# Latent loads split between two blocks, expert rows gathered in the second attention, x quantised beside weight products, row statistics counted with the residual adds: one change to a four-layer decoder on one core

## The reference, cut to what matters

```
x = x + L0_attn(layernorm(x), ...)            # linear attention with decay
x = x + L0_xattn(layernorm(x), ctx_512, ...)  # attention over a latent context
x = x + L0_ffn(layernorm(x), ...)             # reordered, fp8-quantised FFN
x = x + L1_attn(...)                          # selective scan
x = x + L1_xattn(layernorm(x), ctx_512, Wq, w_kc_q, w_kc_kv, W_qr, W_kr, Wo)
x = x + L1_ffn(...)                           # mixture of 8 experts
x = x + L2_attn(...)                          # gated delta rule
x = x + L2_xattn(...)                         # same form as L1_xattn
x = x + L2_ffn(...)                           # 2:4 sparsified FFN
x = x + L3_attn(...)                          # differential attention
x = x + L3_xattn(...)
x = x + L3_ffn(...)                           # shared FFN and 8 experts
```

```
xr = (x / scale)[:, up_index]                     # columns reordered
scale_x = max|xr| per row / 448;  qx = fp8(xr / scale_x)
Wr = W[:, idx];  w_scale = max|Wr| per row / 448;  qw = fp8(Wr / w_scale)
y = qx * scale_x @ (qw * w_scale).T * scale       # gate and up, then down;
                                                  # gate and up outputs are taken at down_index
```

```
q_big = (x @ Wq.T per head) @ w_kc_q              # 128 -> 192 for each head
q_r, k_r = q_big @ W_qr, kv_rope @ W_kr;  attn = softmax(q_r @ k_r.T)
out = ((attn @ kv_rope) @ w_kc_kv.T per head) @ Wo.T
```

## Time and profile before

| | |
|---|---|
| median of 3 runs | 3720.2 us (3717.62 to 3721.66) |
| the profiled execution's own time | 3713.15 us, granted clock 0.84 |
| its span (first to last instruction) | 3711.4 us |
| PE busy | 2790.7 us, 75% of the span |
| PE weight loads | 1860.7 us, 50% (beside PE) |
| DVE busy | 2208.6 us, 60% |
| ACT busy | 1084.3 us, 29% |
| POOL busy | 482.0 us, 13% |
| moved by DMA | 70.29 MB, 19 GB/s on average; 41997 of 85585 packets under 512 B |

### The profile page before, as it was taken

How to read it: one execution, slowest core, us unless ns; L and a number is a source line. 1 busy time by engine, 2 the same in 40 slices (tenths; PEclk the granted TensorE clock), 3 DMA queues, 4 the chain that set the end, 5 groups by cost and what they waited for, 6 DMA issues and landing times. The chain is left out here.

```text
span 3711.4 us, 49035 instructions
## 1 busy us (share of the span) xinstructions
PE 2790.7 (75%) x19853; PEld 1860.7 (50%) x19854; DVE 2208.6 (60%) x4259; ACT 1084.3 (29%) x2461; POOL 482.0 (13%) x321
## 2 busy tenths in 40 slices
PE   4683343649988896698698698695888763898999
PEld 2452321233324564595595695694436742535555
DVE  3555686943369427677677676672494654395233
ACT  2150012510048313233133123221483111384111
POOL 0002000200036222000000000000262000163000
PEclk8896556769999897799799799797799965799899
DMA  5001000040000102000000000004000004001100
GB/s 105 1 1 33 0 3 0 0 107 0 0 1 2 47 0 96 1 1 1 1 1 1 1 2 1 1 1 102 1 2 35 1 16 101 2 2 30 42 1 12
DMA packets 85585, 70.29 MB, mean 19 GB/s; under 512 B 41997, under 2 KB 80334, under 8 KB 84782
## 3 DMA queue, kind: packets, MB, share of 16 engines
q1 hardware_dynamic: 80349, 63.49, 7.0%
q10 hardware_dynamic: 3984, 2.20, 0.3%
q0 software_dynamic: 1024, 1.45, 0.1%
HBM read 56.65 MB, written 4.19 MB: 16 GB/s over the span
## 5 line engine op out<-in xcount | busy, mean ns | idle before, releaser
L1769 POOL TENSOR_SCALAR work<-work,small 128x512 f32<-128x512 f32 x192 | 300.5, 1565 | 1173.0 <-DVE small L1729 1172.9
L1679 PE MATMUL psum<-keysT,arena_a 64*128 64x512 f32 x768 | 237.9, 700 | 65.5 <-ACT work L1793 62.7
L1793 ACT ACTIVATE work<-psum,small 128x512 f32<-128x512 f32 x384 | 261.9, 692 | 73.6 <-DVE small L1723 73.6
L1723 DVE TENSOR_REDUCE small<-psum 128x2 f32<-128x1024 f32 x192 | 230.9, 1204 | 31.2 <-PE psum L1679 25.4
L2867 ACT ACTIVATE work<-psum 128x256 f32<-128x256 f32 x320 | 95.5, 411 | 288.0 <-PE psum L2774 287.0
L1679 PEld LDWEIGHTS psum<-keysT,arena_a 64*128 64x128 f32 x768 | 62.6, 198 | 182.1 <-ACT work L1793 137.3
L2848 DVE TENSOR_TENSOR work<-psum,work 128x256 f32<-128x256 f32 x256 | 108.7, 425 | 74.7 <-PE psum L2802 69.8
L1597 DVE TENSOR_TENSOR arena_a<-psum,work 96x512 f32<-96x512 f32 x96 | 62.8, 681 | 146.0 <-PE psum L1563 146.0
L1346 PE MATMUL psum<-arena_b,arena_a 96*96 96x512 f32 x128 | 94.1, 907 | 72.6 <-DVE arena_b L1375 38.2
L2774 PE MATMUL psum<-consts,work 128*128 128x128 f32 x640 | 83.4, 288 | 76.1 <-DVE work L2839 76.1
L1776 ACT ACTIVATE work<-work,small 128x512 f32<-128x512 f32 x192 | 139.1, 726 | 0.0
(11 more groups left out here) (552 smaller groups left out, 5961.9 us busy)
## 6 DMA issues: line engine op xcount, KB each, us to landing
arena_a<-in_L_xattn_Wo SPq DMA_DIRECT2D x3, 2048.0 KB, 13.2
arena_a<-in_L_xattn_Wq SPq DMA_DIRECT2D x3, 2048.0 KB, 20.8
work<-keys SPq DMA_DIRECT2D x48, 128.0 KB, 5.1
arena_a<-in_L_xattn_w_kc_q SPq DMA_DIRECT2D x3, 1536.0 KB, 16.5
arena_a<-in_L_attn_w_qkv SPq DMA_DIRECT2D x1, 4096.0 KB, 13.6
decay_rows<-work SPq DMA_DIRECT2D x2, 1532.0 KB
arena_b<-in_L_ffn_We_gate_up SPq DMA_DIRECT2D x1, 2816.0 KB
arena_a<-in_L_xattn_W_qr SPq DMA_DIRECT2D x3, 768.0 KB, 4.4
```

The source lines that it names most:

```text
L1679: mm = nc.tensor.matmul(ps[:, m % 2 * 2 + j, :], qT[r:r + DC, i, t * P:(t + 1) * P], k.keysT[r:r + DC, b * SK:(b + 1) * SK], start=True, s ...
L1723: nc.vector.tensor_reduce(top[:, 2 * m:2 * m + 2], ps[:, m % 2 * 2:m % 2 * 2 + 2, :], AX.X, ALU.max, negate=True).then_inc(*maxed.up())
L1769: nc.gpsimd.tensor_scalar(e, e, total[:, 2 * m:2 * m + 1], None, ALU.mult).then_inc(*even_scaled.up())
L1793: last = nc.scalar.activation(probs[m % 4][:, j, :], ps[:, m % 2 * 2 + j, :], ACT.Exp, bias=top[:, 2 * m + j:2 * m + j + 1], accum_out=tot ...
```

## The change

1. **Latent loads.** `latent_attention` issues W_qr, W_kr, w_kc_kv, Wo and w_kc_q in the layernorm's block and the rest (Wq, the sine and cosine tables of layer 1, keys4) in the fold block. keys4 is laid out so that each of its 16 DMAs moves 4 KB runs (32x1024) instead of 256 B runs (32x16x64).
2. **l3_ffn's large loads** ("l3f") are issued in the block of `route`.
3. **Expert rows.** The two short index lists are loaded in L0_xattn's first block and `gather` runs on POOL in L0_xattn's second block; the gathered rows (wgu) lie in arena_a now, the diagonals in arena_b.
4. **x is quantised** by DVE in the weights' block, between L1004 and L1007, and the small block is dissolved into it.
5. **Row statistics** are also counted at the end of L0_attn, L0_xattn, L1_ffn, L2_ffn and L3_attn (`count_rows`, `close_rows`), whose residual adds go by tiles of 256 columns instead of 512 (in three of them), and the layernorms behind them are `counted`. ACT loads the square root's table ahead of time at the end of L0_xattn, L1_ffn and L2_ffn.

```diff
+def count_rows(k, dve, added, t):
+    dve.wait_ge(*added.at(t + 1))
+    row_stats(k, t).then_inc(*k.sig("rowed").up())
+
+def close_rows(k, dve):
+    dve.wait_ge(*k.sig("rowed").at(NT))
+    for t in range(NT):
+        k.nc.vector.bn_aggr(k.ln_mv[:, t, :], k.ln_two[:, t, :])
...
@@ def l0_xattn(k, lists, gather):
+        @block.sync
+        def _(sp):
+            lists(sp)
...
+        @block.gpsimd
+        def _(pool):
+            gather(pool)
...
+        @block.scalar
+        def _(act):
+            nc.scalar.activation(k.ln_rs[:, 1, 0:1], k.c["one"], ACT.Sqrt)
...
-            for b in range(B):
+            for t in range(NT):
+                b = t // 2
                 dve.wait_ge(*mm_out.at(b + 1))
-                nc.vector.tensor_tensor(x[:, 2 * b:2 * b + 2, :], x[:, 2 * b:2 * b + 2, :],
-                                        ps[:, b, :].rearrange("p (t d) -> p t d", t=2), ALU.add)
+                nc.vector.tensor_tensor(x[:, t, :], x[:, t, :], ps[:, b, t % 2 * D:(t % 2 + 1) * D],
+                                        ALU.add).then_inc(*added.up())
+                if t >= 1:
+                    count_rows(k, dve, added, t - 1)
+            count_rows(k, dve, added, NT - 1)
+            close_rows(k, dve)
...
@@ l1_ffn, behind each residual add of the last expert
+                if e == E - 1:
+                    dve.wait_ge(*added.at(g + 1))
+                    row_stats(k, t).then_inc(*k.sig("rowed").up())
+            close_rows(k, dve)
...
@@ l0_ffn
-    diag = A.take(P, 18, P)
-    wgu = Bq.take(FP, 2 * FT, D)
+    wgu = A.take(FP, 2 * FT, D)
+    diag = Bq.take(P, 18, P)
...
+            k.link(dve, nc.vector.tensor_tensor(xm, xn[:, :, :], mask_up..., ALU.mult), "dve")
+            k.link(dve, nc.vector.tensor_reduce(sx, xm, AX.X, ALU.max, apply_absolute_value=True), "dve")
...
+            quantise(k, dve, xm, xt, qx)
             dve.wait_ge(*mm.at(3))
+            nc.vector.tensor_copy(scale_row2.rearrange("p (a b) -> p a b", a=2), ps[:, 4:6, 384:384 + P])
...
@@ latent_attention
-    keys4 = W.take(P, B, 16, DC)
+    keys4 = W.take(P, 4, 16, DC)
...
+        load(k, sp, tag + "_d", [(w_qc, ...)])
+
+    def issue_rest(sp):
+        load(k, sp, tag + "_q", [(wq, io[n + "Wq"].rearrange("(h k) i -> k h i", h=H))])
...
-        load(k, sp, "keys4", [(keys4[32 * a:32 * a + 32, :, c:16:4, :], k.keys[32 * c:32 * c + 32].rearrange(
-            "p (b n) d -> p b n d", b=B)) for a in range(4) for c in range(4)])
+        load(k, sp, "keys4", [(keys4[32 * a:32 * a + 32, c], k.keys[32 * c:32 * c + 32]) for a in range(4) for c in range(4)])
...
     with k.block() as block:
+
+        @block.sync
+        def _(sp):
+            issue_rest(sp)
...
-def route(k, w_router, before, after, weights, tmp, wname, over_all):
+def route(k, w_router, before, after, weights, tmp, wname, over_all, issue=None):
...
-            interleave, counted = stage in ("L0_attn", "L0_xattn", "L1_ffn"), stage in ("L1_ffn", "L2_ffn", "L3_ffn")
+            interleave = stage in ("L0_attn", "L0_xattn", "L1_ffn")
+            counted = stage not in ("L0_attn", "L1_attn", "L1_xattn", "L2_xattn")
```

More of the change, by code:

```diff
@@ L1049, in _ @@
                                      column(t, FP), start=True, stop=True)
+            for t in range(2):
+                m = nc.tensor.matmul(ps[:, 4 + t, 384:384 + P], k.c["ones"], column(16 + t, P), start=True, stop=True)
             m.then_inc(*mm.up())
[L1053 to L1064, removed]
     Bq.reset(), W.reset()
-    qx = W.take(P, NT, D, dt=BF16)
-    xm, xt = Bq.take(P, NT, D), Bq.take(P, NT, D)
-    qxT, xpick = Bq.take(P, 2, N, dt=BF16), Bq.take(P, 2, N, dt=BF16)
-    sx, rx = k.small[:, 0:NT], k.small[:, 8:8 + NT]
+    qxT, xpick = W.take(P, 2, N, dt=BF16), W.take(P, 2, N, dt=BF16)
     turned = k.sig("turned")
@@ L1838, in route, with _ @@
     with k.block() as block:
+        if issue:
+            @block.sync
+            def _(sp):
+                issue(sp)
         @block.tensor
@@ L2044, in _ @@
                     sparsify(i - 1)
+    added = k.sig("added")
     with k.block() as block:
+        @block.scalar
+        def _(act):
+            nc.scalar.activation(k.ln_rs[:, 1, 0:1], k.c["one"], ACT.Sqrt)
         @block.tensor
@@ L2084, in l3_ffn @@
     yield issue
-    route(k, w_r, before, after, weights[:, :, 1:9], tmp, "l3f_r", over_all=True)
+    route(k, w_r, before, after, weights[:, :, 1:9], tmp, "l3f_r", over_all=True, issue=issue_rest)
     up, silud, hid, down, added = (k.sig(s) for s in ("proj", "silud", "hid", "mm_out", "added"))
@@ L3143, in program @@
         for stage in STAGES:
[L3144 to L3145 removed]
+            interleave = stage in ("L0_attn", "L0_xattn", "L1_ffn")
+            counted = stage not in ("L0_attn", "L1_attn", "L1_xattn", "L2_xattn")
+            if stage == "L0_attn":
                 layernorm(k, interleave)
[L3147 to L3154 removed]
+                l0_attn(k)
+            elif stage == "L0_xattn":
+                layernorm(k, interleave, counted=counted)
+                run = l0_ffn(k)
+                l0_xattn(k, *next(run))
+            else:
+                if stage != "L0_ffn":
+                    run = SUBLAYERS[stage](k) if stage in SUBLAYERS else latent_attention(k, stage)
+                layernorm(k, interleave, next(run), counted)
+                for _ in run:
+                    pass
         gone = k.sig("gone")
```

102 lines of the change are left out of this document (48 added, 54 removed).

## The result

The changed kernel took 3615.32 us, the median of 3 runs (3608.78 to 3625.04), against 3720.2: a ratio of 0.972, 95% interval 0.969 to 0.976. The forecast was 3600 with a range of 3585 to 3615. The direction was right, and 104.9 us were saved where 119.5 were forecast. The runs now lie 16 us apart, before 4. The profiled execution took 3615.32 us itself, its span 3613.5: 97.9 less than the span before.

What follows compares the result with a forecast made beforehand. Blocks' ends, held by POOL's gather and SP's load issues, kept PE, DVE and ACT standing. Terms summed to 119.5 us saved: 3713.15 profiled became 3593.7, with the 7.05 offset 3600.7, stated as 3600; range 3585 to 3615.

Steps and rivals of the forecast that it cites:

- both at the clock they had: L2_xattn, after w_kc_q lands: the two stretches up to the queries take 10.58 and 15.79 us, at their earlier clock.
- terms 5 and 6: L2_xattn and L3_xattn: folds start earlier, then wait for w_kc_q; 25.6 and 24.1 us saved.
- term 2: L0_ffn's layernorm freed of POOL's gather: 27.7 us saved, the gather covered by 111.90 us of idle POOL in L0_xattn.
- Term 1: Row statistics counted ahead of layernorms: 2.0 us saved in each of three places, 2.4 in one, 0.8 in another.
- Rival B: L0_xattn: POOL's issues and DVE get in each other's way, 24 us, giving 3624 us; chance 0.06.
- The rule that I weighed there: At the moved gather: DVE copy or tensor_scalar in a two-port mode and GpSimd lock each other out of shared ports.
- Term 3: L0_ffn: x quantised by DVE during its wait for the weight products, 15.7 us saved.
- Term 4: L1_xattn: fold starts after the layernorm, then waits for Wq; 19.5 us saved, after 1.8 for the clock (bounds 0 and 2.5).
- Term 7: L3_ffn: router starts 7.2 us earlier, but the stall moves to the large block's loads; saving -0.3 us.
- The offset of 7.05 us: Whole kernel: the median lies 7.05 us above the profiled execution, so 3593.7 becomes 3600.7.

Runs made afterwards that it cites:

- latents_only: The kernel before with only the latent loads split and the keys in 4 KB runs: 3654.72 us, ratio 0.984.
- after_again: The changed kernel run once more without an edit: 3629.39 us, ratio 0.976.
- gather_paced: The changed kernel with POOL waiting after each of the 16 indirect DMAs of expert rows until its data has landed: 3610.35 us, ratio 0.971.
- l3f_split: The changed kernel with L3_ffn's Ws loads issued in the layernorm, its We loads in the router's block with their own wait: 3620.1 us, ratio 0.974.
- gather_twice: The changed kernel with the 16 indirect DMAs of expert rows issued twice, with a wait between: 3647.79 us, ratio 0.982.
- stats_only: The kernel before with only the row statistics counted with the residual adds and the table loaded ahead: 3726.37 us, ratio 1.0026.

## Why the prediction was right or wrong, by its steps

The direction and the waits were right; some prices were not. For the 3615.32 us measured first, whose trace has no stretch, the step that failed is the price of the products behind the new waits, "both at the clock they had" (terms 5 and 6). For the runs near 3630 it is also term 2's free cover.

- **Term 1**: from the start of the last block's PE work to the square root L0_xattn takes 11.81 us instead of 13.83, 2.0 as forecast. Behind L0_attn it is 12.84 instead of 13.94: 1.1 for 2.0, since PE's last products there took 9.53 us for 8.93. L2_ffn and L3_attn together gained 1.1 (0.8). L1_ffn gained 2.5 (2.4), but that is no proof: it stands at 135.95 in latents_only, which does not count its rows, and at 133.50 in after_again.
- **Term 2**: L0_ffn starts within 0.3 us of the forecast. The step that failed is the cover: "their new block has 111.90 us in which POOL does nothing" counted POOL's time, not what its DMAs do to PE: 15 to 24 us in five of six traces, 18.0 of them in after_again, none in the first. **Rival B** had the right place and size (24 us) under a wrong mechanism, and a chance of 0.06: luck. The rule that I weighed there speaks of DVE. The Trainium skill, SBUF — State Buffer, section "Who interferes with whom", names DVE and GpSimd as sharing ports and DMA as sharing none. DVE's mean was 0.57 us for one instruction in L0_xattn's second block with the stretch and 0.58 without, and in the stretch itself DVE had nothing running, so that lock was not what held the block; PE, which the page sets apart from DMA's ports, was held. My evidence against B, equal times in the layernorm, could not have shown it: PE does almost nothing there beside POOL.
- **Term 3**: L1121 starts at 411.77, 0.5 later than forecast relative to L0_ffn's start, and the first product behind it took 2.50 us instead of 1.35. 15.7 was 14.1. In gather_paced, with the same code here, L0_ffn took 195.03 instead of 196.06, so 1.0 of the 1.6 is this execution's.
- **Term 4**: from the square root to the queries 18.3 saved instead of 19.5: Wq's wait ended 0.2 us later than forecast, and the clock cost 2.8 in L1519, above its upper bound of 2.5.
- **Terms 5 and 6**: the waits are there as forecast, the savings are not: 20.8 for 25.6; L2_ffn, L3_attn and L3_xattn together 20.1 for 24.9. The failed step is "10.58 and 15.79, both at the clock they had". L1501 ran partly at 2.4 GHz before (granted clock 0.76 and 0.79 over its 9.45 and 9.14; 7.70 at 0.94, 13.92 at 0.50), and PE had been busy for 10 us ahead of it. In L2_xattn it now stands behind a wait of 5.30 and runs at 0.50. In L3_xattn the waits are 2.60, 0.75 and 0.94, and the clock is low from the fold's start. That is 4.5 and 3.1 us. In L3_xattn w_kc_q also landed 22.25 us after the square root, some 2 later than the forecast has it. I had added a price for the clock in term 4 and left it out here.
- **Term 7**: L3_ffn took 0.34 more, forecast 0.3; the new wait was 10.0 instead of 7, with the router faster by its clock (5.24 for 6.96). l3f_split shows that the stall had moved and could be taken away.
- **Unchanged code** was put at nothing. L2_attn took 9.1 us more than in the trace before, L0_attn 2.1 more where 2.0 less were forecast. The offset of 7.05 us between median and profiled execution covers about half of that in the forecast of the median: 3720.2 - 119.5 is the 3600.7. So the 21.6 us missing from trace to trace are 14.6 from median to median.

For a kernel without the stretch gather_paced is the test, at 3610 us; forecast were 3600. What its trace prices directly is 4.4 and 2.9 us in the two products and 1.0 in L1's above its 1.8, some 8 of the 10. The split is not exact: its sublayers lie from 2.7 us under (L1_ffn) to 5.2 over (L2_attn) what before less the terms would give. From 3610 to the 3629 of after_again it is mostly the stretch (L0_xattn 164.24 for 147.11). That the first three runs lay at 3609 to 3625 fits a mixture (the profiled one had none), but only profiled executions show which had it.

What stays open is the mechanism of the stretch, and why it came in five of the six profiled executions with the 16 indirect DMAs issued once, unpaced and at their place or later, and not in the first (it came on both chips on which such kernels ran later; which chip the first ran on is not on record). The semaphore records narrow it. In these five and in gather_twice updates by PE come up to 12.4 to 14.7 us after their matmuls' recorded ends, those by DVE and ACT never more than 0.2 us (a few left no record). In before and in the first trace PE's are never later than that either, and in the four traces with a wait after each row DMA at most 2.5, beside the eight DMAs of one column, which are not paced. What holds PE's updates no run shows.

## What to carry to other kernels

Idle time of POOL is not free cover for a gather: beside a dense stream of small matmuls, wait for each indirect DMA before the next, or leave it where PE is idle. An engine that stands still may have its work ready: compare the end of what releases it with its start. When a wait moves, price every PE step behind it at both clocks, not only the first that comes to mind. One trace per kernel hides some 5 us of this kernel's own spread (L2_attn alone took 1144.5 to 1153.6), so compare sublayers over several traces before naming a loss, and a gain inside a sublayer with the sublayer's end before counting it.

## What the hardware showed that I had not expected

- Indirect DMAs of 88 rows of 1 KB, 1.29 us apart, hold back PE's instructions: 57 matmuls in 22 us against 176 in 16. With 3.05 us between them, and with plain DMAs of the same shape, L0_xattn takes 146.9 to 149.3 us, with none it takes 146.2 (stats_only).
- In such a stretch other engines hear of PE's matmuls late: DVE began 9.67 us after the recorded end of the matmuls it waited for, against 0.03 in the first trace.
- The granted clock can be low while PE is busy without a break: L1537 had 64 matmuls of 64 columns with PE busy 13.87 of 14 us, at 0.50, and its equals took 13.89 us in every one of the 17 traces. In before the clock fell from 1.0 to 0.5 in the middle of the 64-column products (L1501 of L2_xattn ran at a mean of 0.76, L1510 behind it at 0.50).
